# Inter-chunk decays of a Mamba-2 layer read from tables, intra-chunk exponents packed into row groups, and y computed in one block

## The reference, cut to what matters

```python
proj = einsum('bsd,ed->bse', x, in_proj_w)            # gate, hs, B, C, dt
hBC = silu(causal_conv4(hBC)); dt = clip(softplus(dt + dt_bias), 0, 100)
xch = hs * dt; A_dt = dt * A; A_cum = cumsum(A_dt)    # within a chunk of 128
L = exp(segsum(A_dt))
Y_diag = einsum('bzlhn,bzshn,bhzls,bzshp->bzlhp', Cc, Bc, L, xch)
decay_states = exp(A_cum[..., -1:] - A_cum)
states = einsum('bzlhn,bhzl,bzlhp->bzhpn', Bc, decay_states, xch)
Y_off = einsum('bzlhn,bzhpn,bhzl->bzlhp', Cc, prev, exp(A_cum))
y = Y_diag + Y_off + hs * D;  g = y * silu(gate)
out = groupwise_rms_norm(g) * norm_w @ out_proj_w.T
```

## Time and profile before

| | |
|---|---|
| median of 3 runs | 1862.39 us (1862.04 to 1862.73) |
| profiled execution | 1863.36 us, its span 1861.6 us |
| mean granted TensorE clock | 0.986 |
| busy shares PE, DVE, ACT, POOL | 97%, 67%, 49%, 54% |
| one step in the middle of the kernel | 16.37 us |

### The profile page before, as it was taken

The page is one execution under the profiler, slowest core; times in us unless marked ns, Lnnn a source line. Parts: engine busy times, 40 slices in busy tenths (PEclk is TensorE's granted clock), DMA queues, the critical chain, the costliest instruction groups (busy, mean ns, idle before and its releaser), DMA issues.

```text
span 1861.6 us, 35838 instructions
## 1 busy us (share of the span) xinstructions
PE 1805.1 (97%) x10520; PEld 1448.8 (78%) x10520; DVE 1256.5 (67%) x2147; ACT 918.5 (49%) x1660; POOL 1006.2 (54%) x812
## 2 busy tenths in 40 slices
PE   5799999999999999999999999999999998999998
PEld 4577887788777877787778777887788776788886
DVE  6588728872887377746884688457754884877776
ACT  4466526652665256635663566346644663222221
POOL 4266645664566446654665366546654657633430
PEclk9899999999999999999999999999999997999999
DMA  2211101110111011101120111001101111111101
GB/s 93 63 53 41 46 3 45 52 52 0 47 53 52 0 47 51 53 0 36 46 64 6 29 53 53 17 29 53 47 23 30 42 35 53 40 52 35 51 17 46
DMA packets 49019, 74.94 MB, mean 40 GB/s; under 512 B 10356, under 2 KB 18676, under 8 KB 48984
## 3 DMA queue, kind: packets, MB, share of 16 engines
q1 hardware_dynamic: 47976, 73.12, 12.9%
q10 hardware_dynamic: 1008, 1.38, 0.2%
HBM read 70.35 MB, written 4.06 MB: 40 GB/s over the span
## 4 chain that ended last, share of the span: by engine, by line
PE 94%; DVE 2%; POOL 1%; issue 1%; ACT 1%; POOLq 0%; DVEq 0%; ACTq 0%
PE proj L758 16%; PE proj L760 16%; PE proj L759 16%; PE y L891 7%; PE y L945 6%; PE y L947 6%; PE y L946 6%; PE y L881 4%; PE trb L858 3%; PE diff L867 3%; PE y L758 2%; PE y L760 2%; PE y L759 2%; PE misc L867 1%; PE misc L931 1%
## 5 line engine op out<-in xcount | busy, mean ns | idle before, releaser
L758 PE MATMUL proj<-xhi,w_hi 128*128 128x512 f32 x1088 | 466.1, 428 | 5.4 <-DVE v L1068 5.4
L760 PE MATMUL proj<-xhi,w_lo 128*128 128x512 f32 x1088 | 426.2, 392 | 0.0
L759 PE MATMUL proj<-xlo,w_hi 128*128 128x512 f32 x1088 | 425.5, 391 | 0.0
L406 POOL TENSOR_TENSOR w_lo<-w_raw,w_hi 128x512 fp32r<-128x512 f32 x144 | 184.1, 1297 | 227.5 <-ACT w_hi L536 227.5
L1068 DVE SCALAR_TENSOR_TENSOR v<-proj,par_sb,v 128x510 f32<-128x510 f32 (+2 forms) x384 | 282.1, 742 | 14.9 <-ACT v L558 11.6
L758 PEld LDWEIGHTS proj<-xhi,w_hi 128*128 128x128 f32 x1088 | 205.0, 188 | 75.5 <-issue 7.9
L462 POOL TENSOR_TENSOR g_lo<-gated,g_hi 128x512 fp32r<-128x512 f32 x128 | 163.8, 1283 | 182.1 <-ACT g_hi L689 182.0
L760 PEld LDWEIGHTS proj<-xhi,w_lo 128*128 128x128 f32 x1088 | 204.8, 188 | 46.5
L759 PEld LDWEIGHTS proj<-xlo,w_hi 128*128 128x128 f32 x1088 | 205.4, 189 | 38.6
L1163 DVE TENSOR_TENSOR M<-diff,cb 128x512 f32<-128x512 f32 x256 | 170.4, 686 | 82.2 <-ACT diff L644 82.2
L945 PE MATMUL y<-wo_hi,g_hi 128*128 128x512 f32 x512 | 202.9, 396 | 4.0 <-POOL g_lo L462 4.0
(11 more groups left out here) (179 smaller groups left out, 3420.1 us busy)
## 6 DMA issues: line engine op xcount, KB each, us to landing
w_raw<-in_win SPq DMA_DIRECT2D x144, 256.0 KB, 2.7
wo_raw<-in_wout SPq DMA_DIRECT2D x64, 256.0 KB, 2.6
M<-in_w SPq DMA_DIRECT2D x14, 512.0 KB, 3.7
cb<-in_w SPq DMA_DIRECT2D x7, 512.0 KB, 3.4
row_l<-rows_l SPq DMA_DIRECT2D x192, 6.0 KB
out<-resid SPq DMA_DIRECT2D x8, 256.0 KB, 2.0
rows_l<-gated SPq DMA_DIRECT2D x9, 128.0 KB, 2.5
resid<-in_x SPq DMA_DIRECT2D x4, 256.0 KB, 4.7
```

Of the source, the lines that this page charges most:

```text
L406: e.tensor_tensor(w_lo[:, slot, i, :], w_raw[:, i, :], w_hi[:, slot, i, :].bitcast(F32), ALU.subtract).then_inc(split.sem, 1)
L758: e.matmul(o, hi_l, hi_r, start=first, stop=False)
L759: e.matmul(o, hi_l, lo_r, start=False, stop=False)
L760: return e.matmul(o, lo_l, hi_r, start=False, stop=last)
```

## The change

- `M` gets two slots more. The decay of the pair (chunk 1, chunk 0) is now a product of two factors: `fade_l` = exp(A_cum of the later chunk), loaded for each tile and head from a DRAM table as a row broadcast to 128 partitions, and `fade_s`, a per-partition number for each head and batch made once. DVE's `weigh_past(head)` multiplies `fade_l`, `fade_s` and C·B, in four instructions of 128x128, eight a tile.
- The two kinds within a chunk have four exponent matmuls a tile instead of six for three kinds. Each contracts 15 rows, held at partitions 0, 32, 64 or 96; the two heads of a kind fill a two-bank tile `decay[z]`, which ACT passes over in two instructions of 128x1024 (Relu, then Exp) and DVE in one (`weigh_own(z)`).
- `y` is one block at the end of PE's step. PE's order is: unit 0, turn(0), turn(1), units 1, 2, 3, the exponents of the next tile, y. The transposes go to the banks of y. ACT exponentiates the next tile after the last gate tanh and ahead of the wo_hi copy (L672).
- DVE's order is: weigh_past(0), weigh_past(1), weigh_own(0), times_dt(0), times_dt(1), conv_rest(0) with weigh_own(1) behind its first multiply-add, conv_rest(1) with hs_silu(0) inside, hs_silu(1), both gate_silu, ysum.
- `sq` has one half instead of two, and POOL alternates square and sum.
- Ahead of the loop, B and C are projected first; fewer parts of the sums are stored. SP issues 8 row transfers and 2 broadcasts a tile instead of 4.

```diff
             def step(g, j, par_, nxt, nxt2, ahead):      # PE
                 def turn(h):
                     pe.wait_ge(silu.sem, silu.at(g, j, h - 1) if par_ else silu.at(g, j, 0))
-                    pe.wait_ge(xdts.sem, xdts.at(g, j, h))
+                    pe.wait_ge(ysum.sem, ysum.at(g, j, h - 1))
+                    pe.wait_ge(oadded.sem, oadded.at(g, 0, 0))
...
-                turn(0)
-                exponents(0)
-                exponents(1)
                 if nxt:
                     unit(0)
+                turn(0)
                 turn(1)
-                exponents(2)
-                exponents(3)
                 if nxt:
                     unit(1)
-                y_first()
-                exponents(4)
-                exponents(5)
-                if nxt:
                     unit(2)
                     unit(3)
-                y_second()
+                if ahead:
+                    exponents(g, j + 1, 1 - par_)
+                y()
```

```diff
+            def exponents(g, j, par_):
+                pe.wait_ge(mdone.sem, mdone.at(g, j, 0))
+                pe.wait_ge(s_rowq[par_], (TPG * 64) * g + 64 * j + (128 - 64 * par_))
+                pe.wait_ge(cbd.sem, cbd.at(g, 0, 0))
+                for z in range(2):
+                    for head in range(2):
+                        first = 32 * (2 * z + head)
+                        mm = e.matmul(decay[z][:, head * HALF:(head + 1) * HALF],
+                                      row_l[first:first + PARTS + PARTS * B, par_, :],
+                                      row_r[first:first + PARTS + PARTS * B, par_, :], start=True, stop=True)
+                    mm.then_inc(dready.sem, 1)
...
+            def decays(g, j):                            # ACT
+                for z in range(2):
+                    act.wait_ge(dready.sem, dready.at(g, j, z + 1))
+                    e.activation(decay[z][:, :], decay[z][:, :], ACT.Relu, scale=-1.0).then_inc(dbound.sem, 1)
+                for z in range(2):
+                    act.wait_ge(dbound.sem, dbound.at(g, j, z + 1))
+                    e.activation(decay[z][:, :], decay[z][:, :], ACT.Exp, scale=-1.0).then_inc(edone.sem, 1)
...
                 if nxt:
                     gate_tanh(gate[:, 1 - par_, :], 1, ready.at(g, j, 4))
+                if ahead:
+                    decays(g, j + 1)
                 act.wait_ge(woscaled.sem, woscaled.at(g, j, 1))
                 e.copy(wo_hi[:, bass.ds(j, 1), :].rearrange("p a f -> p (a f)"), wo_raw[:, :])\
                     .then_inc(wohi.sem, 1)
...
+                def weigh_past(head):                    # DVE
+                    dve.wait_ge(s_fade[head], (16 * TPG) * g + 16 * j + 16)
+                    dve.wait_ge(cbd.sem, cbd.at(g, 0, 0))
+                    dve.wait_ge(yready.sem, yready.at(g, j, 0))
+                    for b in range(B):
+                        cols = slice(b * P, (b + 1) * P)
+                        ins = e.scalar_tensor_tensor(
+                            M[:, 4 + head, cols], fade_l[:, head, cols],
+                            fade_s[:, bass.ds(2 * t + head, 1), b:b + 1].rearrange("p a b -> p (a b)"),
+                            cb[:, 1, cols], ALU.mult, ALU.mult)
+                    ins.then_inc(mdone.sem, 1)
+                def weigh_own(z):
+                    dve.wait_ge(edone.sem, edone.at(g, j, z + 1))
+                    e.tensor_tensor(M[:, 2 * z:2 * z + 2, :], decay[z][:, :].rearrange("p (a f) -> p a f", a=2),
+                                    cb[:, 2 * z:2 * z + 1, :].broadcast_to([P, 2, HALF]), ALU.mult)\
                         .then_inc(mdone.sem, 1)
                 w = tile_weights(t + 1)
+                weigh_past(0)
+                weigh_past(1)
+                weigh_own(0)
                 times_dt(0)
-                weigh(0)
-                weigh(1)
                 times_dt(1)
                 if nxt:
-                    conv_rest(0, w, tap.at(g, j, 1), convs.at(g, j, 0),
-                              (lambda: weigh(2), lambda: weigh(3)))
+                    conv_rest(0, w, tap.at(g, j, 1), convs.at(g, j, 0), (lambda: weigh_own(1),))
```

More of the change, by code:

```diff
@@ L312, in _, with step @@
             load_rows(0, 0)
-            def step(g, j, par_, nxt, nxt2):
+            def step(g, j, par_, nxt, nxt2, ahead):
                 sp.wait_ge(wolo.sem, wolo.at(g, j, 0))
@@ L648, in step @@
+            decays(0, 0)
+            def step(g, j, par_, nxt, nxt2, ahead):
                 w = tile_weights(TPG * g + j + 1)
@@ L807, in first_unit @@
                 pair, piece, h = n // 4, (n // 2) % 2, n % 2
-                free = (None, None, 1, 2, None, None, 3, 4)[n]
-                project(pair, piece, h, 2 * pair + piece + 1, free, bc_banks[0][piece] if pair else proj)
+                free = (None, None, None, None, 1, 2, 3, 4)[n]
+                project(1 - pair, piece, h, 2 * pair + piece + 1, free, (diff, proj)[piece])
             dt_turned = (trb, misc)
@@ L1115, in _ @@
             link(e.scalar_tensor_tensor(dtq, dtv, 0.0, dtq, ALU.max, ALU.add))
+            for h in range(2):
+                hs_silu(bc[:, 0, :], h, h + 1)
             dt_flat = dt[:, :, :].rearrange("p t f -> p (t f)")
@@ L1121, in _ @@
                 .then_inc(s_dta, 1)
-            conv_rest(1, w, 2, 2)
-            hs_silu(hs[:, 0, :], 0, 1)
-            hs_silu(hs[:, 0, :], 1, 2)
-            gate_silu(gate[:, 0, :], 0, 3)
-            gate_silu(gate[:, 0, :], 1, 4)
-            bc_tile(0, 0, 2, 4, 4, bc_banks[0][0])
-            bc_tile(0, 1, 2, 4, 4, bc_banks[0][1])
+            w = bc_weights(0, 1)
+            conv_rest(0, w, 3, 4, banks=bc_banks[0][1])
+            conv_rest(1, w, 4, 6, banks=bc_banks[0][1])
+            for h in range(2):
+                hs_silu(bc[:, 1, :], h, h + 3)
+            w = tile_weights(0)
+            conv_rest(0, w, 5, 8, banks=diff)
+            conv_rest(1, w, 6, 10, banks=diff)
+            for h in range(2):
+                hs_silu(hs[:, 0, :], h, h + 5)
             def cbs_kept(ncb):
@@ L1142, in _, with step @@
             cbs_kept(1)
-            def step(g, j, par_, nxt, nxt2):
+            gate_silu(gate[:, 0, :], 0, 7)
+            gate_silu(gate[:, 0, :], 1, 8)
+            dve.wait_ge(s_fade_s, 1)
+            def step(g, j, par_, nxt, nxt2, ahead):
                 t = TPG * g + j
```

355 lines of the change are left out of this document (161 added, 194 removed).

## The result

The changed kernel takes 2251.35 us (2250.61 to 2252.52, four runs); the kernel before took 1862.22 us beside it (1861.70 to 1862.73, four runs). The ratio is 1.209, with a 95% interval of 1.207 to 1.211. The profiled execution has a span of 2249.3 us and a mean granted clock of 0.912 (before: 1861.6 and 0.986).

A forecast was written before the change was run, and what follows sets the result against it. It took PE's work to bound the old step (16.37 us), with DVE near binding. 55 steps x 7.7 plus 8 x 1.6, less 11 ahead of the loop, gave 425 over 1863.4: 2288, say 2285; range 1945 to 2400.

The forecast's parts named there:

- the mechanism that it gave the highest chance: Four or five weighings blocked by POOL and the clock falling in most steps; 2170 to 2400 us, chance 0.50.
- DVE sets unit 2 behind E: DVE ends conv_rest(0) at E + 8.7, so unit 2 starts at 8.85, 2.4 us after PE is free.
- E: The moment when y of the last tile is done on PE and the next step begins.
- The weighings and POOL: Four of eight weigh_past each wait for a POOL instruction, so they end at E + 6.7 instead of 3.15.
- Unit 2 and the idleness: With weighings blocked, unit 2 starts at E + 12.4, with PE idle for 5.95 us.
- The clock falls: After 5.95 us idle, PE runs 5.3 us at half speed and loses 2.65 us in units 2 and 3.
- The step: Steps 1 to 7 with a next tile, 55 of them, take 24.05 us, 7.7 more than before.
- The steps 0: The eight steps after a window, with POOL's burst over, cost 1.6 us more each, 13 in all.
- The exponents: Four exponent matmuls on PE, in different array rows, take 0.4 us; bounds 0.22 (full overlap) and 0.86 (none).
- Ahead of the loop: Projecting B and C first removes PE's 11.1 us idle before C·B; gain 11 us, bounds 0 and 15.
- SP's longer queue at nothing: SP's ten transfers a step instead of four, with later weights queued behind weigh_past, cost nothing unless steps were again 16 us.
- The faster rival: PE stays the bound with a 15.5 us step, 69 us less, 1795; needs conv_rest(0) by E + 6.5; chance 0.07.

The follow-up runs named there:

- e2: The changed kernel with the eight weigh_past moved behind conv_rest(1) and SP loading the next weights before fade_l; 1988.08 us.
- e4: The changed kernel with the eight weigh_past products left out in every step, their slots of M zeroed once; 1980.86 us.
- e1: The changed kernel with one wait added: POOL starts its burst only when the next tile's eight weigh_past are done; 2009.29 us.
- e8: e7 without POOL's wait for weigh_past; 2090.75 us.
- e5: The changed kernel with 14 extra 128x512 matmuls, never read, on PE between units 1 and 2; 2179.36 us.
- e11: e9 with all four exponent products at partition 0, where they can't overlap (wrong decays); 1855.09 us.
- e6: e1 with SP's queue reordered: input weights, then fades, ahead of the raw output weights, rows last; 1977.18 us.
- e9: e7 with turns behind unit 1, times_dt behind the second convolution pair, and POOL's weight splits waiting for both silu products; 1814.90 us.
- e7: e6 with DVE doing conv_rest(0) before times_dt, then conv_rest(1), then weigh_own(1); 1859.53 us.
- e10: e9 without POOL's wait for the silu products; 1815.33 us.
- e3: The changed kernel with all four exponent matmuls using the row group at partition 0 (wrong decays); 2365.44 us.

## Why the prediction was right

The forecast was 2285 us with a range of 1945 to 2400; 2251 is 1.5% below it, by the mechanism that it gave the highest chance. Its steps, one by one:

- **DVE sets unit 2 behind E.** Right. In step 0, with nothing in its way, unit 2 is at E + 8.89 (1047.82 less 1038.93), where 8.85 was predicted, after 2.29 us of idleness (2.4). But the sum came out right with a limit missing: it ran over DVE's instructions alone, and e2 and e4 show a second limit close by. The turns come behind unit 0 and hold times_dt, so that without the weighing unit 2 is at 8.2 and later all the same.
- **The weighings and POOL.** Right, and shown by e1 and e8: a wait on POOL brings the mean from 736 or 738 to 345 or 347 ns. POOL's start was E + 1.9 (predicted 1.8), DVE's E + 0.7 (0.9). Three weighings are blocked in 41 of the steps and five in 14, where the prediction had four in all. In the step shown they end at E + 6.0 instead of E + 6.7. (The prediction's own terms, 1.8 and 1.3 + 1.0 + 1.0 + 0.8 and four times 0.15, add up to 6.5.) It did not see that two steps of seven would be worse.
- **Unit 2 and the idleness.** The mean over the 55 steps is E + 12.3 (predicted 12.4) and 5.76 us (5.95). That this is so close is in part luck: it is the mean of steps at 11.7 and steps at 14.06, for which the prediction had one value between.
- **The clock falls.** Right, in all 55 steps. But units 2 and 3 take 7.8 us in the mean, from 6.9 to 8.6, where 5.6 + 2.65 = 8.25 was predicted; with the idle time filled (e5) they take 5.8. So the fall costs 2.0 a step and not 2.65.
- **The step** is 23.27 in the mean, against 24.05. Of the 0.78 less, 0.5 are the units behind the wait and the exponents, 0.16 is y (2.84, not 3.0) and 0.08 is unit 2's start. In 55 steps that is 43 us.
- **The steps 0** were put at 1.6 more each, 13 in all. The clock falls in five of the eight, which the prediction left open for waits of 2.4 us but did not count here; with their windows they cost 22.6 (20.1, and 2.5 for the first). This hides 10 of the 43 us, so the forecast was nearer than its terms.
- **The exponents** 0.32, not 0.4; the upper bound of 0.86 was too low, it is 0.96 (e11). The 0.12 us a product that the prediction read for y is that of a pair: rows 3 have 16 in 1.09.
- **Ahead of the loop** some 16 us (84.00 less 67.79) and not 11. PE's wait for C·B did not go; it is 5.34 us instead of 11.14.
- **SP's longer queue at nothing**: right in the changed kernel, where ACT waited for w_raw only 28.6 us in all. It cost 32 us as soon as the step was shorter (e1 against e6).
- **The faster rival** (1795, if conv_rest(0) were over by E + 6.5) needed "DVE to do them 2.2 us faster". It needed another order instead: e9 has unit 2 at 6.9 us behind the end of y (917.99 less 911.06), the step at 15.8, and 1814.9 us.

What the 389 us are made of: the meeting with POOL, with the fall of the clock that follows from it, is 242 us (e1), and 274 with SP's queue mended (e6). What is left to the kernel before is 115 us (e6), already net of the 14 gained ahead of the loop. It goes with DVE's order between the end of y and the convolutions, for e7 takes away 118 us with the order alone. How much of the last is clock (e6 0.971, e7 0.992) and how much waiting was not separated.

## What to carry to other kernels

- When a table or a factor replaces an exponent, look at where the new operands lie. Eight short DVE instructions with two SBUF inputs were put beside a burst of POOL, and each that met it took about a us more; one wait that moves POOL behind them was worth 242 us, because POOL had slack.
- A block that moves off the path takes its cover along. Write out the loop "end of y, sums, weighing, convolution, unit 2" in the new order before moving y; moving two turns and two scalings was worth 44 us (e7 to e10) with no instruction removed.
- When a step comes down, every queue behind it must be read again: SP's order was free at 23 us a step and cost 32 us at 18.

## What was not expected of the hardware

- The clock also fell behind waits of 2.0 to 2.5 us (e6, and the steps 0 of the changed kernel), in some steps and not in others: in e6 units 2 and 3 took 5.86 us at 1.00 behind a wait of 2.50, and 7.28 at 0.77 behind one of 2.04. What decides between the two was not found.
- The cost of a meeting hangs on tenths: POOL 0.6 us earlier against y made the weighings 1.9 us longer (e3). DVE 0.45 us later, where its sequencer goes back to the top of a loop, did the same in 14 steps of the changed kernel.
- Filling PE's wait with fourteen matmuls for nothing paid, by 72 of the 126 us that I had put on it (e5).
